# Scalar operations of the vector engine rewritten in fused or two-tensor form, in a four-layer gated cross-attention stack

## The reference

```
def _layernorm(x, axis=-1, eps=1e-05):
    m = jnp.mean(x, axis=axis, keepdims=True)
    v = jnp.var(x, axis=axis, keepdims=True)
    return (x - m) / jnp.sqrt(v + eps)

x = x + jnp.tanh(g_xattn[l]) * xattn_l(_layernorm(x), ctx_1024, ...)
x = x + jnp.tanh(g_ffn[l]) * ffn_l(_layernorm(x), ...)
```

```
def fp4_quant_dequant(x):
    xb = x.reshape(shape[:-1] + (shape[-1] // BLOCK, BLOCK))      # BLOCK = 16
    scale = jnp.max(jnp.abs(xb), axis=-1, keepdims=True) / 6.0
    scale = jnp.maximum(scale, jnp.float32(1e-12))
    xn = xb / scale
    idx = jnp.searchsorted(_MID, jnp.abs(xn))
    q = _GRID[idx] * jnp.sign(xn) * scale
    return q.reshape(shape)
```

## Time and profile before

| | us |
|---|---|
| median of 3 runs | 904.48 |
| lowest and highest | 901.93 and 909.58 |
| the profiled execution's own time | 905.73 |
| span in its profile | 903.9 |
| busy: PE, DVE, ACT, POOL | 661.5, 600.6, 297.5, 306.7 |
| mean granted clock of TensorE | 0.821 of full speed |

### The profile page before, as it was taken

How to read it: one execution, slowest core, us unless ns; L and a number is a source line. 1 busy time by engine, 2 the same in 40 slices (tenths; PEclk the granted TensorE clock), 3 DMA queues, 4 the chain that set the end, 5 groups by cost and what they waited for, 6 DMA issues and landing times.

```text
span 903.9 us, 10008 instructions
## 1 busy us (share of the span) xinstructions
PE 661.5 (73%) x2926; PEld 402.9 (45%) x2926; DVE 600.6 (66%) x1429; ACT 297.5 (33%) x547; POOL 306.7 (34%) x602
## 2 busy tenths in 40 slices
PE   5558754665656999988389894137878788898996
PEld 4323322343434666546144342014334556666774
DVE  7555666998854345447755555765557797997976
ACT  2125232221120333523104342011445545444553
POOL 8101221345551211115414342241022454554543
PEclk8559677678677899979659897555889999999999
DMA  8656221000013242200504521021510132232432
GB/s 243 149 126 174 50 66 27 0 1 0 1 36 91 68 127 51 69 19 1 169 6 140 142 55 42 0 81 39 168 49 4 48 95 95 77 116 74 132 97 69
DMA packets 67990, 67.72 MB, mean 75 GB/s; under 512 B 25119, under 2 KB 48223, under 8 KB 67552
## 3 DMA queue, kind: packets, MB, share of 16 engines
q1 hardware_dynamic: 66976, 65.85, 26.5%
q10 hardware_dynamic: 960, 1.23, 0.4%
HBM read 50.29 MB, written 17.60 MB: 75 GB/s over the span
## 4 chain that ended last, share of the span: by engine, by line
PE 42%; DVE 29%; issue 10%; DMA 7%; POOL 6%; ACT 3%; SPq 2%; POOLq 0%; DVEq 0%; ACTq 0%
PE ps L1392 6%; PE ps L1440 6%; PE ps L1420 5%; POOL sg L608 5%; DVE mraw L1048 4%; DVE xn L921 3%; DMA QG<-q_parts 2%; PE ps L1356 2%; DVE st L907 2%; PE ps L1578 2%; PE ps L1373 2%; PE ps L1569 2%; DMA q_parts<-loT 2%; PE ps L1616 1%; PE ps L1617 1%
## 5 line engine op out<-in xcount | busy, mean ns | idle before, releaser
L1048 DVE TENSOR_REDUCE mraw<-ps 128x4 f32<-128x308 f32 x256 | 116.1, 476 | 105.5 <-PE ps L1392 44.4
L682 ACT ACTIVATE PT<-ps 110x512 f32<-110x512 f32 x192 | 111.6, 596 | 183.1 <-PE ps L1420 91.1
L1392 PE MATMUL ps<-KG,QG 98*128 98x308 f32 x256 | 111.8, 475 | 51.3 <-DVE mraw L1048 30.1
L608 POOL TENSOR_TENSOR sg<-sg,cb 128x512 f32<-128x512 f32 x64 | 88.6, 1386 | 84.7 <-ACT sg L802 80.4
L1420 PE MATMUL ps<-QG,KG 128*110 128x512 f32 x192 | 96.8, 519 | 17.5 <-DMA QG<-mT 12.3
L1392 PEld LDWEIGHTS ps<-KG,QG 98*128 98x128 f32 x256 | 60.9, 243 | 101.2 <-DVE mraw L1048 65.7
L537 POOL TENSOR_TENSOR nt<-nhv,rs 128x4 f32<-128x4 f32 (+1 forms) x102 | 25.1, 246 | 184.9 <-DVE rs L914 179.1
L1233 DVE TENSOR_TENSOR loT<-hc,hiT 128x512 fp32r<-128x512 f32 x72 | 80.6, 1119 | 0.7 <-ACT hiT L786 0.6
L1440 PE MATMUL ps<-PT,VN 128*18 128x512 f32 x512 | 75.1, 661 | 0.0
L786 ACT ACTIVATE hiT<-hc 128x512 fp32r<-128x512 f32 x72 | 45.5, 632 | 87.1 <-DVE hc L1246 51.8
L481 POOL CAST mhl<-mraw 128x64 fp32r<-128x64 f32 x16 | 4.8, 301 | 197.9 <-DVE mraw L1048 186.8
(11 more groups left out here) (255 smaller groups left out, 1432.2 us busy)
## 6 DMA issues: line engine op xcount, KB each, us to landing
cb<-c_parts SPq DMA_DIRECT2D x64, 256.0 KB, 3.2
QG<-q_parts SPq DMA_DIRECT2D x48, 256.0 KB, 3.9
KG<-k_parts SPq DMA_DIRECT2D x48, 154.0 KB, 3.0
q_parts<-hiT SPq DMA_DIRECT2D x16, 256.0 KB, 2.3
q_parts<-loT SPq DMA_DIRECT2D x16, 256.0 KB, 2.1
k_parts<-kmH SPq DMA_DIRECT2D x16, 154.0 KB, 2.4
k_parts<-kmL SPq DMA_DIRECT2D x16, 154.0 KB, 2.5
VN<-v_parts SPq DMA_DIRECT2D x16, 144.0 KB, 2.6
```

Source lines behind the costliest of these rows:

```text
L608: pool.tensor_tensor(sg[:, n % 2, :], sg[:, n % 2, :], cb[:, k % CRING, :], ALU.mult).then_inc(sc_done, 1)
L682: act.activation(PT[0:w, q % PTR, :], ps[0:w, 4 + q % 2, :], ACT.Exp, scale=SCALE[l]).then_inc(exp_done, 1)
L1048: dve.tensor_reduce(mraw[:, n % 2, i, g * HG:(g + 1) * HG], ps[:, u % 2, 0:GK].rearrange("p (h k) -> p h k", k=K), AX_X, ALU.max).then_inc ...
L1392: ins = pe.matmul(o, QG[0:KS, n % 3, g, q], KG[0:KS, n % 3, g, :], start=True, stop=l not in (1, 2))
```

## The change

quant4: the scale (L839) and the magic number (L844) become scalar_tensor_tensor, with the second constant read from a one-column tensor that is broadcast; the bitwise and (L843) becomes a tensor_tensor with a broadcast column of integers; the small reduction of the reciprocal (L841) is dropped and its factor goes into L842, which becomes a scalar_tensor_tensor. statistics: nhv (L912) becomes a scalar_tensor_tensor, var (L913) a tensor_tensor, each with a broadcast column. apply (L921): the tensor_scalar with two pointer scalars becomes a scalar_tensor_tensor with the mean as pointer scalar and the reciprocal root, one column broadcast over 128 elements, as second tensor. The columns are written by five memsets and waited for at the start of DVE's stream. quant8, the residuals and L914 stay as they are.

```diff
--- before.py
+++ after.py
@@ -143,6 +143,9 @@
         qw = sb("qw", [P, 2, S])
         qs = sb("qs", [P, 2, 44])
         hscale = sb("hscale", [P, 2, 44])
+
+        cf = sb("cf", [P, 4])
+        ci = sb("ci", [P, 1], I32)
         am = sb("am", [P, 16])
         w8 = sb("w8", [P, P])
         w8b = sb("w8b", [P, P], BF16)
@@ -254,7 +257,7 @@
         y3_ready, yT3_ps, dw_hi, dw_lo = sem("y3_ready"), sem("yT3_ps"), sem("dw_hi"), sem("dw_lo")
         c_out = [sem(f"c_out{b}") for b in range(B)]
         cb_in = [sem(f"cb_in{r}") for r in range(CRING)]
-        hq_scaled = sem("hq_scaled")
+        hq_scaled, cf_set = sem("hq_scaled"), sem("cf_set")
         am_w_part, am_w_all = sem("am_w_part"), sem("am_w_all")
         f3_step, ld_down, ld_ffn1, o_zero = sem("f3_step"), sem("ld_down"), sem("ld_ffn1"), sem("o_zero")
 
@@ -834,14 +837,15 @@
 
                 v = lambda k: (qw if work is None else work)[0:n, k, 0:nb * 16].rearrange("p (b e) -> p b e", e=16)
                 s3 = lambda k: scale if k == 0 and scale is not None else qs[0:n, k, 0:nb]
-                bc = lambda k: qs[0:n, k, 0:nb].unsqueeze(2).to_broadcast([n, nb, 16])
+                bc = lambda k: s3(k).unsqueeze(2).to_broadcast([n, nb, 16])
+                const = lambda c: c.unsqueeze(2).to_broadcast([n, nb, 16])
                 link(dve.tensor_reduce(s3(0), src, AX_X, ALU.max, apply_absolute_value=True))
-                link(dve.tensor_scalar(s3(0), s3(0), 1.0 / 6.0, 1e-12, ALU.mult, ALU.max))
+                link(dve.scalar_tensor_tensor(out=s3(0), in0=s3(0), scalar=1.0 / 6.0, in1=cf[0:n, 1:2].to_broadcast([n, nb]),
+                                              op0=ALU.mult, op1=ALU.max))
                 link(dve.reciprocal(s3(1), s3(0)))
-                link(dve.tensor_scalar(s3(1), s3(1), 1.0 - 2.0 ** -22, None, ALU.mult))
-                link(dve.tensor_tensor(v(0), src, bc(1), ALU.mult))
-                link(dve.tensor_scalar(v(1).bitcast(I32), v(0).bitcast(I32), EXP_BITS, None, ALU.bitwise_and))
-                ins = dve.tensor_scalar(v(1), v(1), 1.0, 1.5 * 2.0 ** 22, ALU.max, ALU.mult)
+                link(dve.scalar_tensor_tensor(out=v(0), in0=src, scalar=1.0 - 2.0 ** -22, in1=bc(1), op0=ALU.mult, op1=ALU.mult))
+                link(dve.tensor_tensor(v(1).bitcast(I32), v(0).bitcast(I32), const(ci[0:n, 0:1]), ALU.bitwise_and))
+                ins = dve.scalar_tensor_tensor(out=v(1), in0=v(1), scalar=1.0, in1=const(cf[0:n, 2:3]), op0=ALU.max, op1=ALU.mult)
                 if work is not None:
                     return ins
                 link(ins)
@@ -909,8 +913,9 @@
                 for i in tiles:
                     ins = dve.bn_aggr(mv[:, i, :], st[:, i, :])
                 link(ins)
-                dve.tensor_scalar(nhv[:, s], mv[:, s, 1], EPS, -0.5, ALU.add, ALU.mult)
-                link(dve.tensor_scalar(var[:, s], mv[:, s, 1], EPS, None, ALU.add))
+                dve.scalar_tensor_tensor(out=nhv[:, s], in0=mv[:, s, 1], scalar=EPS, in1=cf[:, 0:1].to_broadcast([P, TPB]),
+                                         op0=ALU.add, op1=ALU.mult)
+                link(dve.tensor_tensor(var[:, s], mv[:, s, 1], cf[:, 3:4].to_broadcast([P, TPB]), ALU.add))
                 dve.tensor_scalar(rs[:, s].bitcast(I32), var[:, s].bitcast(I32), -0.5, RSQRT_GUESS,
                                   ALU.mult, ALU.add).then_inc(stats_ready, 1)
 
@@ -918,7 +923,8 @@
 
                 dve.wait_ge(rstd_ready, LN_ORDER.index((n, b)) + 1)
                 for i in range(b * TPB, (b + 1) * TPB):
-                    ins = dve.tensor_scalar(xn[:, i, :], src[:, i, :], mv[:, i, 0:1], rs[:, i:i + 1], ALU.subtract, ALU.mult)
+                    ins = dve.scalar_tensor_tensor(out=xn[:, i, :], in0=src[:, i, :], scalar=mv[:, i, 0:1],
+                                                   in1=rs[:, i:i + 1].to_broadcast([P, D]), op0=ALU.subtract, op1=ALU.mult)
                 return ins
 
             def normalise_batch(stage, b):
@@ -1265,6 +1271,10 @@
                 hidden_low(NS - 1)
                 residual(B - 1)
 
+            for k, value in enumerate((-0.5, 1e-12, 1.5 * 2.0 ** 22, EPS)):
+                dve.memset(cf[:, k:k + 1], value)
+            dve.memset(ci[:, :], EXP_BITS).then_inc(cf_set, 1)
+            dve.wait_ge(cf_set, 1)
             dve.memset(QG[96:P, 0, :, :].bitcast(F32), 1.0).then_inc(ones_set, 1)
             dve.wait_ge(ld_x[0], 16)
             statistics(x, 0)
```

## The result

The changed kernel takes 910.4 us (median of 20 runs, 902.7 to 916.6) against 904.3 for the kernel before (20 runs, 899.0 to 917.0). The ratio is 1.0062, 95% interval 1.0042 to 1.0082: 5.6 us longer, 3.8 to 7.4. The forecast was 6.3. It is under the 1% that was called the line of no change, but clear of the noise of so many runs.

The account below looks back on a forecast made before the run. DVE was taken to carry the chain in the first feed-forward block, though no engine bounds the whole. Terms 4.2 + 0.3 + 0.1 + 0.1 + 0.7 + 0.6 + 0.3 = 6.3 us on 904.5 gave 910.8 us, range 903 to 917.

Parts of the forecast that it names:

- The bound and the place: First feed-forward block: DVE carries the chain through the quantiser; its idle time comes behind L1148 and covers none of it.
- cover rival: Quantiser's growth vanishes behind PE or POOL, only L921 counts: about +1.3 us, 905.8 us; chance 0.10.
- The price of the new forms: Fused form without a pointer costs a two-tensor operation: 158 ns plus 1.04 ns an element; a broadcast costs nothing.
- surcharge rival: The fused form itself costs 60 ns more in L839, L842, L844 and L912: 914.6 us; chance 0.18.
- The hidden quantiser: First feed-forward block, 704 elements, 8 times: +0.530 us each, +4.2 us, all on the chain.
- The input quantisers beside POOL: Two in the first feed-forward block: dropped L841's wait passes to the next line, together +0.1 us.
- lock rival: New forms don't contend with POOL in the first feed-forward block: 19.3 us released, 891.5 us; chance 0.06.
- Normalising: L921: free groups +0.045 us each, +0.7 on the chain; contended groups +0.6 in first feed-forward block, +0.3 elsewhere.
- +0.2 a group: Normalising groups beside POOL in the first feed-forward block: longer streaming remains behind released locks, +0.6 us for three.
- Start and statistics: L912, L913: nothing; 0.2 us less if two-input forms skip the memset wait and L914 bears it. Start memsets: hidden.
- Layer-0 attention by under 1: The layer-0 attention stage would get longer by under 1 us.
- the last rival: PE's granted clock shifts in the first feed-forward block: 3 us either way; chance 0.06 shared with repeated loss of lock.

Follow-up runs that it names:

- part_rate: Kernel before with only the scale, bitwise and and magic number in the new forms, small reduction kept: ratio 1.0093, +8.4 us (5.6 to 11.3).
- part_apply: Kernel before with only the normalising instruction L921 changed to its fused form: ratio 1.0002, +0.2 us (-1.7 to 2.2).
- part_quant: Changed kernel with statistics and normalising (L912, L913, L921) back in their old form: ratio 1.0040 against the kernel before, +3.6 us (1.0 to 6.1).

## Why the prediction was right

- **The bound and the place.** That DVE carries the chain in the first feed-forward block, and that its idle time lies behind the quantiser and covers nothing, held: part_rate's +8.4 us is, within its interval, the growth of its instructions counted one by one (8.2), and the cover rival is out. One reading was wrong without touching the sum: DVE doesn't idle for 7.5 us behind L1148. It computes the residual's statistics until 211.79 and idles 3.22 us, until ACT's fsg; the chain doesn't pass through those statistics.
- **The price of the new forms**, equal to a two-tensor operation without the pointer: exact (204, 425 and 892 ns). The surcharge rival is out.
- **The hidden quantiser**, +0.53 us a turn: measured 0.53.
- **The input quantisers beside POOL**, one wait handed on to the next line: seen in the trace, 4.82 us where 4.80 was worked out. The lock rival is out: the groups of L926 beside POOL's operations still lose three waits.
- **Normalising was mis-sized.** The free group grew from 1.11 to 1.13 us where 0.045 was forecast, and the group beside POOL from 5.25 to 5.33 where it was 0.2:

```profile
120.65 1.13 DVE L926 SCALAR_TENSOR_TENSOR xn<-x,mv,rs 128x128 f32<-128x128 f32 x4
...
224.67 5.33 DVE L926 SCALAR_TENSOR_TENSOR xn<-x,mv,rs 128x128 f32<-128x128 f32 x4
224.71 1.67 POOL L590 TENSOR_TENSOR qh<-qh 128x704 f32<-128x704 f32 x1 [5.21 <-DVE qh L848]
226.46 1.67 POOL L591 TENSOR_TENSOR qh<-qh 128x704 f32<-128x704 f32 x1
```

The step that failed is "+0.2 a group": I counted the longer streaming behind each of three releases. POOL's next operation starts 80 ns behind its last and keeps its 1.67 us, so it isn't pushed back by the tail of the instruction between. The 67 ns don't add up: the first instruction of the group took 1.86 us for 1.79, the second and third what they took before, so the tail counts once a group. The other groups that met POOL grew by 0.06 to 0.22 us, some 0.1 on average. With 15 x 0.02 + 3 x 0.08 and the other contended groups at 0.1, the term is 0.9 instead of 1.6, and the sum 5.6. That is the measured ratio's figure, by some luck, since its interval is 3.6 us wide. part_apply (+0.2, -1.7 to 2.2) can't tell 0.9 from 1.6.
- **Start and statistics.** Nothing that can be told apart, as forecast: the wait beside the memset moved to L919, whose end at 8.54 instead of 8.75 us is the 0.2 that the prediction gave for this case, and DVE's five small memsets ended at 1 us, ahead of x's transfer. "Layer-0 attention by under 1" isn't borne out by this trace: its last statistics lie 1.8 us behind (160.90 against 159.10). But part_apply's trace is 1.7 behind there with a ratio of 1.0002, and part_quant's 0.2, so one trace doesn't settle it.
- **The clock** moves single turns by 1.5 us, as the last rival allowed, but the medians stayed inside the range.

## What to carry to other kernels

A tensor_scalar on f32 in SBUF ran at 0.52 ns an element where tensor_tensor and scalar_tensor_tensor ran at 1.04, so writing a constant as a tensor doubles the streaming part: worth it only where it removes a whole instruction, as the fused reciprocal does (-0.22 us each; 3.7 us in all by the traces, 3 to 7 by the runs), never one for one. Take such edits apart before judging them: this change was one good edit, worth 3 us or more, under the forms with half the rate (+8.4). And where two engines lock each other out, moving or dropping the instruction that waits hands the wait to the next one of its kind; put beside the other engine's long operations what the trace shows unheld, here operations that read PSUM, maxima and the two BATCH_NORM instructions; the small operations on the variance behind those are held (L912 1.38 us, L914 1.36).

## What the runs showed that was not expected

Beside POOL's memset a two-input instruction of DVE isn't held at all (0.16 us where the one-source form took 1.82), though beside POOL's arithmetic it is held like the other (L916 at 213.18: 1.38 us, as L912 before). An instruction of DVE released by POOL can stream some 70 ns into POOL's next operation without delaying it: L926's first ended 148 ns behind L590, L591 started 79 ns behind it and took its usual 1.67 us. And the four instructions of a normalising group hardly notice the halved rate (start to start 257 ns before, 262 after), though each overlaps the next by some 80 ns (341 and 346 ns long). By the two lines the rate is worth 66 ns at 128 elements, and one pointer less returns 55 of them.
